# Layer tile: layer norm per token with one column of statistics, mask as two half-array products, values moved ahead of the scores

## What is computed

```python
for i in range(DEPTH):                       # 6
    x = attn_layer(shift_tokens(x), Wqkv[i], q_scale[i], k_scale[i], Wo[i]) + x
    x = ffn_layer(shift_tokens(x), ln_g[i], ln_b[i], W1[i], b1[i], W2[i], b2[i]) + x
# attn_layer: 16 heads of 64; q, k scaled to unit length, rotary; each window of 32 queries
#   sees 64 keys (its own window and the one before); sim * 8, masked, softmax, @ v, @ Wo
# ffn_layer:
mu = x.mean(-1, keepdims=True)
var = ((x - mu) ** 2).mean(-1, keepdims=True)
xn = (x - mu) / jnp.sqrt(var + 1e-05) * g + bln
a, gate = jnp.split(xn @ W1 + b1, 2, -1)
return a * jax.nn.gelu(gate, approximate=False) @ W2 + b2
```

## Time and profile before

| | |
|---|---|
| median of three executions | 4724.15 us (4722.18 to 4735.0) |
| the profiled execution | 4729.9 us, span 4728.0 us |
| PE busy, share of the span | 4220.1 us, 89% |
| DVE, ACT, POOL busy | 80%, 71%, 58% |
| mean granted clock of TensorE | 0.942 |
| layer stage | from about 1490 us to 4690 us of the span |

### The profile page before, as it was taken

The page is one execution under the profiler, slowest core; times in us unless marked ns, Lnnn a source line. Parts: engine busy times, 40 slices in busy tenths (PEclk is TensorE's granted clock), DMA queues, the critical chain, the costliest instruction groups (busy, mean ns, idle before and its releaser), DMA issues. The chain is left out here.

```text
span 4728.0 us, 193017 instructions
## 1 busy us (share of the span) xinstructions
PE 4220.1 (89%) x74452; PEld 3406.3 (72%) x74465; DVE 3795.1 (80%) x6502; ACT 3363.7 (71%) x5951; POOL 2753.7 (58%) x3197
## 2 busy tenths in 40 slices
PE   7889976697366899999999999999999999999997
PEld 4444433376254788878887888888887888888886
DVE  5777755644336899989999999989999999999995
ACT  4555521255134789979988899888998889888995
POOL 3222213634324677767776777767776777677772
PEclk8989878799677999999999999999999999999998
DMA  3000004252221211121111111121112111121111
GB/s 154 1 0 0 0 0 121 90 189 84 88 76 45 54 44 42 49 59 50 43 45 55 52 49 43 43 67 43 48 43 61 48 46 45 44 66 44 49 42 38
DMA packets 141887, 255.23 MB, mean 54 GB/s; under 512 B 34160, under 2 KB 56944, under 8 KB 137072
## 3 DMA queue, kind: packets, MB, share of 16 engines
q1 hardware_dynamic: 133520, 235.49, 17.0%
q0 software_dynamic: 8192, 17.84, 1.2%
HBM read 70.76 MB, written 44.04 MB: 24 GB/s over the span
## 5 line engine op out<-in xcount | busy, mean ns | idle before, releaser
L2566 POOL TENSOR_TENSOR d_rc<-d_rc,d_rs 128x512 f32<-128x512 f32 x768 | 964.0, 1277 | 463.0 <-DVE d_rs L2649 447.6
L2576 POOL TENSOR_TENSOR d_rc<-d_rc,d_inv 128x1024 f32<-128x1024 f32 x384 | 722.9, 1903 | 128.2 <-DVE d_inv L2670 127.9
L2132 PE MATMUL d_pair<-d_W_high,d_xs_high 128*128 128x512 f32 x1152 | 519.1, 451 | 117.4 <-issue 34.4
L2649 DVE TENSOR_TENSOR d_rc<-d_pair,d_rot 128x512 f32<-128x512 f32 x768 | 527.5, 687 | 93.7 <-ACT d_sq L2381 75.7
L2381 ACT ACTIVATE d_sq<-d_pair 128x512 f32<-128x512 f32 x768 | 435.2, 596 | 138.9 <-PE d_pair L2132 133.8
L2649 DVE TENSOR_TENSOR d_rs<-d_pair,d_rot 128x512 f32<-128x512 f32 x768 | 522.1, 680 | 0.0
L2132 PE MATMUL d_pair<-d_W_high,d_xs_low 128*128 128x512 f32 x1152 | 461.4, 401 | 0.0
L2132 PE MATMUL d_pair<-d_W_low,d_xs_high 128*128 128x512 f32 x1152 | 460.7, 400 | 0.4 <-issue 0.4
L2659 DVE TENSOR_REDUCE d_ss<-d_sq 128x16 f32<-128x1024 f32 x384 | 448.2, 1208 | 0.0
L2279 PE MATMUL d_pair<-d_OT,d_Wo 128*128 128x128 f32 x3072 | 380.7, 278 | 0.0
L2176 PE MATMUL d_pair<-d_ident,d_rc 128*128 128x128 f32 x3072 | 367.5, 273 | 1.0 <-ACT d_sq L2381 1.0
(11 more groups left out here) (378 smaller groups left out, 11104.5 us busy)
## 6 DMA issues: line engine op xcount, KB each, us to landing
d_VW<-d_V SPq DMA_DIRECT2D x768, 128.0 KB
d_VW<-d_V SPq DMA_DIRECT2D x576, 64.0 KB
leaf_rows<-a_zeros SPq DMA_DIRECT2D x12, 1152.0 KB, 14.6
q_xrow<-leaf_rows SPq DMA_DIRECT2D x24, 576.0 KB
leaf_out<-q_yrow SPq DMA_DIRECT2D x24, 512.0 KB
d_W_whole<-Wqkv_dram SPq DMA_DIRECT2D x7, 1536.0 KB, 6.4
f_xrow<-leaf_rows SPq DMA_DIRECT2D x8, 576.0 KB, 3.6
b_table<-q_w_dram SPq DMA_DIRECT2D x4, 1024.0 KB, 8.0
```

Source lines behind the costliest of these rows:

```text
L2132: mm = nc.tensor.matmul(target, x_part[:, t.par, :], w_part[:, c, :], start=n == 0, stop=n == 2)
L2566: nc.gpsimd.tensor_tensor(own[:, :, a, :], own[:, :, a, :], other[:, :, 1 - a, :], ALU.add).then_inc(s[f"add{qk}_ready"], 1)
L2576: nc.gpsimd.tensor_tensor(heads(rc[:, t.par, half, :]), heads(rc[:, t.par, half, :]), inv[:, t.par, half, :].unsqueeze(2).to_broadcast([12 ...
L2649: ins = nc.vector.tensor_tensor(heads(target), heads(ps[:, j, :]), rot[:, t.par, half, cs, :].unsqueeze(1).to_broadcast([128, HP, DH]), AL ...
```

## The change

The centring product exchanges its operands, so that its result has tokens on partitions. The square on ACT sums each row as it goes (`accum_out`), into one column; `variance` and its product are gone. The root (now right behind its table load) and the reciprocal are of one column; xh is the product with a scalar per partition. A new part on PE, `normalised_turned`, turns xh back (one transpose, between those of the queries and those of the keys), and ACT applies g and b on its way out of PSUM, between its copies of the queries and the keys; xn has two buffers now. `attention_turned` waits for xn of the tile two ahead, where it waited for xh.

The mask is made of 64 rows: a one-hot of 64 rows as weights (`mask_rows`) and a mask of 64 rows as data, both there twice, so that the product for one bank reads partitions 0 to 63 and that for the other 64 to 127. The first half of the values is multiplied ahead of `hidden_gate` and the scores instead of between scores and attend. Not shown below: the waits at the start for one memset less, the load of the one-hot in place of the identity, and arguments handed through.

```diff
--- before
+++ after
@@ -1919,16 +1918,17 @@
-        std = sb("d_std", [128, 128])
-        rstd = sb("d_rstd", [128, 128])
+        xsq_sum = sb("d_xsq_sum", [128, 1])
+        std = sb("d_std", [128, 1])
+        rstd = sb("d_rstd", [128, 1])
...
-        xn = sb("d_xn", [128, 128])
+        xn = sb("d_xn", [128, 2, 128])
...
-        var_bank, gate_bank, up_bank = pair[0][:, 1, :], pair[2][:, 1, :], pair[3][:, 0, :]
+        gate_bank, up_bank = pair[2][:, 1, :], pair[3][:, 0, :]
@@ -2181,7 +2181,6 @@
-                wait(pe, "std_ready", t, -4)
@@ -2208,7 +2207,8 @@
-                    nc.tensor.matmul(s_pair[:, odd, :], ident_b[:], mask[:, t.par, :].unsqueeze(1).to_broadcast([128, HP, DH]),
+                    half = slice(64 * odd, 64 * odd + 64)
+                    nc.tensor.matmul(s_pair[:, odd, :], mask_rows[half, t.par, :], mask[half, :].unsqueeze(1).to_broadcast([64, HP, DH]),
@@ -2259,7 +2259,7 @@
-                wait(pe, "xh_ready", t, -2)
+                wait(pe, "xn_ready", t, -2)
@@ -2288,20 +2288,18 @@
-                nc.tensor.matmul(centred_bank[:, 0:128], centre[:], xs2[:], start=True, stop=True).then_inc(s["mean_done"], 1)
-            def variance(t):
-                if not t.live:
-                    return
-                wait(pe, "xsq_ready", t)
-                wait(pe, "on_ready", t, 2)
-                if t.edge:
-                    wait(pe, "std_ready", t, -1)
-                nc.tensor.matmul(var_bank[:, 0:128], mean_w[:], xsq[:], start=True, stop=True).then_inc(s["var_done"], 1)
-            def hidden(W1, ps, done):
+                nc.tensor.matmul(centred_bank[:, 0:128], xs2[:], centre[:], start=True, stop=True).then_inc(s["mean_done"], 1)
+            def normalised_turned(t):
+                if not t.live:
+                    return
+                wait(pe, "xh_ready", t)
+                nc.tensor.transpose(centred_bank[:, 128:256], xh[:], ident[:]).then_inc(s["xht_done"], 1)
+            def hidden(t, W1, ps, done):
...
-                    mm = nc.tensor.matmul(ps[0:HROWS[c], 128 * c:128 * c + 128], W1[:, 128 * c:128 * c + HROWS[c]], xn[:],
+                    mm = nc.tensor.matmul(ps[0:HROWS[c], 128 * c:128 * c + 128], W1[:, 128 * c:128 * c + HROWS[c]], xn[:, t.par, :],
@@ -2351,23 +2349,23 @@
                 queries(tile(0), 0)
                 keys(tile(0), 1)
                 values(tile(1), 1)
-                variance(tile(5))
                 project(tile(4))
                 queries_turned(tile(1))
+                normalised_turned(tile(5))
                 keys_turned(tile(1))
                 hidden_up(tile(6))
                 attention_turned(tile(3))
                 probabilities_turned(tile(2))
+                values(tile(0), 0)
                 hidden_gate(tile(5))
                 scores(tile(1))
-                values(tile(0), 0)
                 attend(tile(2))
 @@ -2447,8 +2445,8 @@
-                wait(act, "var_done", t, -1)
-                nc.scalar.activation(xsq[:], centred_bank[:, 0:128], ACT.Square).then_inc(s["xsq_ready"], 1)
+                wait(act, "std_ready", t, -1)
+                nc.scalar.activation(xsq[:], centred_bank[:, 0:128], ACT.Square, accum_out=xsq_sum[:]).then_inc(s["xsq_ready"], 1)
@@ -2458,19 +2456,19 @@
-                wait(act, "var_done", t)
+                wait(act, "xsq_ready", t)
...
-                nc.scalar.activation(std[:], var_bank[:, 0:128], ACT.Sqrt, bias=eps[:, 0:1]).then_inc(s["std_ready"], 1)
+                nc.scalar.activation(std[:], xsq_sum[:], ACT.Sqrt, bias=eps[:, 0:1], scale=1.0 / 128).then_inc(s["std_ready"], 1)
...
-                wait(act, "xh_ready", t)
-                wait(act, "upa_done", t, -1)
-                wait(act, "upg_done", t, -1)
-                nc.scalar.activation(xn[:], xh[:], ACT.Identity, bias=vecs_n[:, 1:2], scale=vecs_n[:, 0:1]).then_inc(s["xn_ready"], 1)
+                wait(act, "xht_done", t)
+                wait(act, "upa_done", t, -2)
+                wait(act, "upg_done", t, -2)
+                nc.scalar.activation(xn[:, t.par, :], centred_bank[:, 128:256], ACT.Identity, bias=vecs_n[:, 1:2], scale=vecs_n[:, 0:1]).then_inc(s["xn_ready"], 1)
@@ -2493,14 +2491,14 @@
                 exponentials(tile(3))
                 squares_centred(tile(6))
                 load_sqrt(tile(6))
+                deviation(tile(6))
                 squares(tile(1), 1, "k", 1)
-                deviation(tile(6))
                 take_values(tile(2), 1)
                 squares(tile(1), 0, "q", 0)
                 squares(tile(1), 1, "k", 0)
                 take_queries_turned(tile(2))
+                normalised(tile(6))
                 take_keys_turned(tile(2))
-                normalised(tile(6))
                 take_attention_turned(tile(4))
                 take_probabilities_turned(tile(3))
                 lengths(tile(1))
@@ -2717,8 +2714,8 @@
-                wait(dve, "xn_ready", t, -1)
-                nc.vector.tensor_tensor(xh[:], centred_bank[:, 0:128], rstd[:], ALU.mult).then_inc(s["xh_ready"], 1)
+                wait(dve, "xht_done", t, -1)
+                nc.vector.tensor_scalar(xh[:], centred_bank[:, 0:128], rstd[:, 0:1], None, ALU.mult).then_inc(s["xh_ready"], 1)
@@ -2783,13 +2780,16 @@
-    query = np.arange(128)[:, None] % WIN
+    query = np.arange(WIN)[:, None]
...
-    first = seen & ((np.arange(128)[:, None] >= WIN) | (slot >= WIN))
-    mask = np.where(np.stack([first, seen], 1), 0.0, -1e30).astype(mybir.dt.np(BF16))
+    first = seen & (slot >= WIN)
+    mask = np.tile(np.where(np.concatenate([seen, first]), 0.0, -1e30), (2, 1)).astype(mybir.dt.np(BF16))
+    tokens = np.arange(128)
+    row_of = np.stack([tokens % WIN + np.where(tokens < WIN, WIN, 0), tokens % WIN])
+    rows = np.tile((np.arange(2 * WIN)[:, None, None] == row_of[None]).astype(np.float32), (2, 1, 1)).astype(mybir.dt.np(BF16))
...
-    return {"ident": np.eye(128, dtype=np.float32), "rotary": rotary, "window_mask": mask, "centre": centre}
+    return {"ident": np.eye(128, dtype=np.float32), "rotary": rotary, "window_mask": mask, "window_rows": rows, "centre": centre}
```

More of the change, by code:

```diff
@@ L1888, in local_attention_layers @@
         rot = sb("d_rot", [128, 2, 2, 2, DH])
-        mask = sb("d_mask", [128, 2, DH], BF16)
-        ident_b = sb("d_ident_b", [128, 128], BF16)
+        mask = sb("d_mask", [128, DH], BF16)
+        mask_rows = sb("d_mask_rows", [128, 2, 128], BF16)
         ident = sb("d_ident", [128, 128])
         centre = sb("d_centre", [128, 128])
-        mean_w = sb("d_mean_w", [128, 128])
         eps = sb("d_eps", [128, 1])
@@ L1938, in local_attention_layers @@
             v0_ready v1_ready vw_in0 vw_in1 pv_done on_ready ot_done ot_ready proj_done xm_ready xs2_ready
-            mean_done xsq_ready var_done std_ready rstd_ready xh_ready xn_ready upa_done upg_done g_ready h_ready down_done x_ready
+            mean_done xsq_ready std_ready rstd_ready xh_ready xht_done xn_ready upa_done upg_done g_ready h_ready down_done x_ready
             sqrt_loaded gelu_loaded exp_loaded gate_pe gate_pool gate_sp""".split()
@@ L2039, in _ @@
             sp.dma_start(mask[:], dram["window_mask"]).then_inc(s["consts_in"], 16)
-            sp.dma_start(ident_b[:], dram["ident_b"]).then_inc(s["consts_in"], 16)
+            sp.dma_start(mask_rows[:], dram["window_rows"]).then_inc(s["consts_in"], 16)
             sp.dma_start(centre[:], dram["centre"]).then_inc(s["consts_in"], 16)
@@ L2122, in _ @@
             pe.wait_ge(s["consts_in"], 80)
-            pe.wait_ge(s["memset_done"], 6)
+            pe.wait_ge(s["memset_done"], 5)
             def product(t, target, what):
@@ L2316, in hidden_up @@
                     wait(pe, "h_ready", t, -1, HCH)
-                hidden(W1a, up_bank, "upa_done")
+                hidden(t, W1a, up_bank, "upa_done")
             def hidden_gate(t):
@@ L2327, in hidden_gate @@
                     wait(pe, "g_ready", t, -1, HCH)
-                hidden(W1g, gate_bank, "upg_done")
+                hidden(t, W1g, gate_bank, "upg_done")
             def down(t):
@@ L2369, in _ @@
         def _(act):
-            act.wait_ge(s["memset_done"], 6)
+            act.wait_ge(s["memset_done"], 5)
             def squares(t, half, qk, j):
@@ L2512, in _ @@
             nc.gpsimd.memset(eps[:], 1e-5).then_inc(s["memset_done"], 1)
-            nc.gpsimd.memset(mean_w[:], 1.0 / 128).then_inc(s["memset_done"], 1)
             nc.gpsimd.memset(KT[:, :, 0:WIN], 0.0).then_inc(s["memset_done"], 1)
@@ L2517, in _ @@
             nc.gpsimd.memset(VW[:, 0, 0, :], 0.0).then_inc(s["memset_done"], 1)
-            pool.wait_ge(s["memset_done"], 6)
+            pool.wait_ge(s["memset_done"], 5)
             def two_halves(t, target, source, ready):
@@ L2605, in _ @@
             dve.wait_ge(s["consts_in"], 80)
-            dve.wait_ge(s["memset_done"], 6)
+            dve.wait_ge(s["memset_done"], 5)
             def tables(t):
```

## The result

The changed kernel takes **4710.89 us** (4703.76 to 4715.61, 7 executions) against 4723.94 (4721.67 to 4735.0, 7) of the kernel before on the same chip: ratio 0.9967, 95% interval 0.9956 to 0.9979. It is faster, by 13 us where 43 were forecast. (4711 is the number of rival 2, 4712, by coincidence: its mechanism, halves that don't run together, is not there.) The profiled execution took 4715.61 us, its span is 4713.2 against 4728.0: -14.8.

What follows compares the result with a forecast made beforehand. PE's queue at full clock was taken as the bound. Ordinary tiles -50, layer changes +13, start -2 and drain -4 gave -43 us, applied to the median 4724.15: 4681 us, own range 4655 to 4705.

Steps and rivals of the forecast that it cites:

- rival 2: Mask on PE: its two halves don't run together, +0.19 us per tile, 4712 us; chance 0.15.
- PE's own time: PE's queue per tile: -0.11 transpose for variance product, -0.25 values, -0.19 mask, sum -0.55 us if nothing else is late.
- Transpose against variance product: On PE per tile: the variance product (0.22 us) goes, one transpose of xh (0.11) comes, net -0.11.
- wait for xn: PE at turned attention: xn from ACT is seen at +2.58, PE arrives at +2.51; 0.10 us per tile charged with refill.
- rival 4: Mask before the scores: each form change costs 0.42 instead of 0.10 us and halves are serial; slower, 4750 us; chance 0.11.
- the move of the values: First half of the values on PE: 1.05 us behind the scores, 0.70 elsewhere; gain 0.35, of which 0.10 is given back.
- The chain through DVE: From scores' end to rotated q1: PE's second half of the values waits until 5.4 us after; 0.26 lost every second tile.
- rival 1: DVE's chain has more cover (latency 0.1, not 0.27), xn no refill; PE keeps its full 0.54, 4644 us; chance 0.17.
- Rival 3: xh or xn reach PE some 0.25 us later than worked out: +40 us, 4721 us, no change; chance 0.12.
- The layer changes: Turned attention waits 2.7 us for the new vectors; 1.7 for the path plus 0.9 for the clock, five times: +13 us.
- The start: First ten intervals between row maxima, said to be under other limits: -2 us.
- The drain: End of the stage, where DVE waits for the deviation in five tiles: 0.8 us each, -4 us.

Runs made afterwards that it cites:

- the norm alone: Kernel before with only the per-token norm changed (centring product turned, summed squares, one-column deviation and reciprocal, transpose of the normalised tile): 4725.37 us, ratio 1.0003.
- the second profile: The changed kernel run once more unaltered, beside other follow-up kernels: 4709.11 us, 0.9966 of the kernel before.
- the inverse lengths first: Changed kernel with DVE's inverse lengths placed ahead of the row maxima: 4887.65 us, 0.993 of the kernel before on its chip.
- the edge tiles: Changed kernel with the first half of the values back behind the scores in the written-out first and last tiles only: 4902.97 us, 0.9966 of the kernel before.

## Why the prediction was right and where it was wrong

**PE's own time** was right in all terms but one. Transpose against variance product -0.11 and wait for xn +0.08 (charged 0.10): the norm alone gives 0.03 per tile. Mask 0.21 less, change of form 0.09 more: 0.11 to 0.13 per tile, forecast 0.09. The two halves start 3 ns apart and are done in the time of one, so rival 2 is out, and with 0.09 for a change of form so is rival 4. (The working behind it counted the scores double: the code has 64 small products per tile, and the trace's 128 are two instructions for each.) The Trainium skill (TensorEngine Tiling (Array Packing), Key Properties) says that a change of the tiling mode drains TensorE; by that rule a mask with a form of its own pays twice, and the trace agrees, at 0.09 us for the one added.

The term that was mis-sized is the move of the values, 0.35. It took them to hold PE from 3219.19, an estimate of the last score product's place, to 3220.24. Their first product in that tile stands at

```profile
3219.34 0.50 PE L2132 MATMUL d_pair<-d_W_high,d_xs_high 128*128 128x512 f32 x1
```

so they held it 0.90 and not 1.05. In the tiles that PE binds, the values alone save 0.92 of that on the way to the second half of the values and cost 0.70 elsewhere: 0.22.

**The chain through DVE** was right in kind and in size. In the tile that it binds, 5.38 us from the end of the scores to the second half of the values were measured against 5.37, and 10.18 from there to the next end against 10.14; rival 1, more cover, is out. Only part of its wait is at the second half of the values, the rest at `down`. In the tile with the loop's gap it is PE that binds, 5.60 against 5.49 and 10.11 against 10.14, and there the values' term is what is missing. Pairs of 31.28 instead of 31.14, and so -38.4 over the 177 intervals instead of -49.5, make 11 us of the miss. Rival 3 is out: nothing waits for xh, and the 0.08 for xn was charged.

**The layer changes** were forecast at +1.6 for the path and 0.9 for the clock per tile of new vectors, 12.5 in all; +17.0 were measured, 4.5 more. The path was right. In the two tiles that kept full clock, the part up to the second half of the values is 8.7 from the end of the scores (8.6 before), set by DMAs as forecast, and the part behind it 12.9 (forecast 12.8): +1.7. PE waits longer in the first part, 2.8 for 1.7, only because it gets there sooner. What was mis-sized is the clock: the step knew one hole, and there are two, each long enough. In three of the five tiles it fell behind both, and they take 2.8 us more each, 8.4 in all against 4.5. A tile of each kind, columns as in the earlier trace rows:

```profile
2105.70:2127.30 21.60, 15.62 (x346) 13.57 (x345) 14.06 (x25) 15.64 (x29) 11.75 (x15) 1.00 0.22 56
2626.20:2650.50 24.30, 18.57 (x346) 16.46 (x345) 14.12 (x25) 15.73 (x29) 11.72 (x15) 0.86 0.19 50
```

How many of the five tiles fall differs between executions and kernels with the same waits: four in the second profile, all five with the inverse lengths first.

**The start** was the step that failed most: "The first ten intervals, under other limits, -2" was no reading at all, and they cost +10.1 (12.5 in the second profile). What one would have had to read is attend in these ten intervals, which hold nine attends, kernel before, then after (lines):

```profile
L2251 PE MATMUL d_pair<-d_VW,d_PT 64*32 64x64 f32 x864 | 15.7, 233 | 9.6 <-issue 9.6
```

```profile
L2251 PE MATMUL d_pair<-d_VW,d_PT 64*32 64x64 f32 x864 | 16.0, 239 | 15.8 <-issue 15.8
```

The idle time before attend "issue", 9.6 us over nine tiles, is time in which PE waits for no other engine. It grows to 15.8 when attend follows the scores with no large products between, and with the values ahead alone it was the same:

```profile
L2251 PE MATMUL d_pair<-d_VW,d_PT 64*32 64x64 f32 x877 | 16.1, 233 | 17.4 <-issue 17.4
```

Over all 192 tiles the page has 20.5 us of this idle time, so nearly all of it lies in these nine tiles, whose code is written out and runs once. That the order of the code opens it is shown by the edge tiles: with the values back behind the scores in them it is 8.5 again. The clock does the rest. The first nine intervals, kernel before, after, edge tiles only, norm alone, columns as in the earlier trace rows:

```profile
1522.10:1676.50 154.40, 133.79 (x2863) 113.28 (x2864) 125.54 (x191) 116.92 (x194) 106.68 (x125) 0.97 0.22 62
```

```profile
1518.50:1683.00 164.50, 138.05 (x2875) 119.34 (x2883) 121.65 (x191) 116.64 (x201) 106.67 (x126) 0.90 0.21 58
```

```profile
1715.70:1876.70 161.00, 139.15 (x2871) 117.67 (x2879) 121.80 (x190) 117.01 (x202) 107.22 (x126) 0.92 0.22 60
```

```profile
1519.80:1680.00 160.20, 138.06 (x2857) 115.30 (x2858) 121.34 (x191) 116.21 (x200) 106.82 (x125) 0.93 0.21 60
```

Of the +10.1, 5.8 are idle time of PE (26.4 against 20.6) and 4.3 are busy time, at a clock of 0.90 instead of 0.97. The idle time goes with the place of the values (21.9 in the edge tiles' kernel); the busy time stays at 138 to 139 there and with the norm alone. So the norm too brings the clock down at the start; why isn't shown. By parts, +8.8 came with the values alone, +5.8 with the norm alone, +1.8 with the mask alone, together more than the whole has, each from one profile with a scatter of some 5 us.

**The drain** was forecast at -4 and is 0 within its scatter (from the last maximum to the end other kernels take 77 to 83 us). DVE still waits 1.7 to 2.9 us for each deviation, the reciprocal with its product takes 0.54 instead of 1.28 in the last tile, and from there to the last addition to x it is 6.66 instead of 6.04. The forecast took the 0.8 per tile as gained and left out the way behind xh, which is longer now by the transpose; some of PE's products there ran at a lower clock as well, and the two weren't separated.

The account: 11 (the 177 intervals) + 4.5 (layers) + 12 (start) + 4 (drain) - 3.6 (an earlier begin of the stage, outside the change, so luck) = 28, the 28 us between -43 and the -14.8 of the spans.

## What to carry to other kernels

When a change relieves the engine that binds, list the waits that it will reach sooner, and on each issuing queue what stands ahead of what it then waits for: here the place of one DMA issue and one DVE order, worth nothing before the change, are worth 15 and 16 us behind it. With the place of W1g's issue, which wasn't tried without the change, and the edge tiles as before, it is 63 us of the stage. Price holes by what the clock may do behind them, as a range: equal holes cost 0 or 2.8 us here. Cost written-out edge tiles by themselves, since a hole that the loop hides can stand open there, and bring the clock down. Where a change has several parts, time each alone: the smallest one, two half-height masks at once, gave more of the stage than the whole did.

## What the hardware showed that was not expected

- Two large groups of small products (128 each) without larger ones between leave PE idle for "issue" in code that runs once: 1.8 us per tile instead of 1.1. In the loop there is next to none. Why, no run here shows.
- Holes shorter than the 3.58 of the earlier trace rows are enough for the granted clock to fall, and equal ones don't always do it. Before the queries of a layer's tile of new vectors it fell behind 1.7 us in two of five tiles with the norm alone (0.57 over the next 4 us in one) and in none of five in the kernel before, behind 2.5 in five of five with the values ahead alone, and behind 2.7 to 2.8 in three of five in the changed kernel. What decides it, no run here shows.
- ACT's accumulated sum appears as an instruction of its own, 0.2 us:

```profile
3235.95 0.20 ACT L2449 ACTIVATION_READ_ACCUMULATOR d_xsq<-d_pair 128x1 f32 x1
```

- DVE's reciprocal goes with its columns: 0.15 for 128x1, 0.35 for 128x32, 0.94 for 128x128.
